# First attention: a planner's order for TensorE with a charge for changing between rounded and full-precision matmuls, and a hold

## The chip, the cores and the metric

The kernel runs on one core of a Trainium2 chip. The metric is device time in microseconds (us) of one execution, as the median over runs. The core has five engines that each execute their own list of instructions in order and wait for one another through semaphores: TensorE (PE in the profile, with its weight loads as PEld), VectorE (DVE), ScalarE (ACT), GpSimd (POOL) and SyncE (SP), which here issues DMAs.

## The reference

The program is two transformer-like layers over 2048 tokens of 256 features. Six steps follow each other: a routed feed-forward, the first attention, a routed feed-forward, a mixed feed-forward, a second attention, a mixed feed-forward. The change touches only the first attention (latent attention with 16 heads, causal):

```
q = (_rmsnorm(x @ w_q_a, q_a_ln) @ w_q_b).reshape(b, s, H, DQ)
ckv = x @ w_kv_a
...
kv = (_rmsnorm(c_kv, kv_a_ln) @ w_kv_b).reshape(b, s, H, DN + DV)
...
scores = jnp.einsum('bqhd,bkhd->bhqk', qf, kf) * scale
scores = jnp.where(mask[None, None], scores, jnp.finfo(scores.dtype).min)
p = jax.nn.softmax(scores, axis=-1)
o = jnp.einsum('bhqk,bkhd->bqhd', p, v).reshape(b, s, H * DV)
return o @ w_out
```

with s = 2048, H = 16, DQ = 192. The kernel folds the key and value weights into the query and output weights, so that all heads share one key of 128 features (64 latent, 64 rotated) and one value of 64 latent features.

## The kernel before, in words

`latent_heads` (L910) works on the 16 heads as 8 pairs. For each pair the queries are cut into 8 units of 256 queries for both heads, that is 512 columns (`LATENT_UNITS`, with `LATENT_CHUNKS` as the order of the chunks of 512 queries). A unit with number j has j + 1 steps, one for each 256 keys; the last is on the diagonal. Over all units there are 64 units and 288 steps (`LATENT_STEPS`, `FIRST_STEP`).

What happens to a step g:

- `scores`: TensorE computes two key tiles x 512 queries into one of two score banks (two PSUM banks each). Each tile is three products of *rounded* operands (type fp32r, high and low parts: L998, L999, L1003), and on the diagonal a product in bf16 that adds the mask (L1001).
- `max`: VectorE takes the running maximum over the steps of a unit (L1232). `evac`: ScalarE copies the scores to one of 12 held slots in SBUF (`HELD_STEPS`, L1108), which frees the score bank. `scores` of step g waits for `evac` of step g - 2; `evac` of step g waits for `max` of g, and for `values` and `sum` of step g - 12, which leave the slot.
- When all steps of a unit have their scores, TensorE turns the maxima (`turn_max`, L1020), VectorE reduces them (L1268), TensorE spreads them (`spread`, L1027). Then for each step VectorE subtracts them (`add`, L1279), ScalarE takes the exponential (`exp`, L1114), TensorE multiplies with the latent values (`values`, L1014: two matmuls on fp32 data in *full precision*, four records in the trace), and GpSimd adds up the sums (`sum`, L1208).
- After the last step of a unit ScalarE and VectorE drain the output bank; after each second unit TensorE does `sums` (L1033), `turn_sums` (L1039), `spread_inverse` (L1044) and two `project` (L1053), with steps of ScalarE and VectorE between them. All these are full-precision matmuls or transposes of fp32 data.
- `query` (L1062) makes the queries of a chunk for one head: five rounded products. `turn_q`, `turn_kv`, `fold_query` and `fold_out` (L1068 to L1091) make the weights of a pair, 8 times, from what SyncE has loaded.

The kinds in `SIDE` share two PSUM banks in turn.

The order of all this on each engine comes from `latent_plan` (L794). It lists every event with its engine, an assumed duration, a rank (its due time, counted in steps), and the events it waits for. `scores` of step g has rank g, `values` of step g has g + 11 (`SECOND_PASS_AFTER`), `add` and `exp` 10.0 and 10.4 later than g, `query` 7 steps before its first use, the weights 22 steps before. `turn_max`, `spread`, `sums`, `turn_sums`, `spread_inverse`, `project` and the drains have rank -1000 (`urgent`). Then it plays the work through: for each engine it looks for the earliest time at which any waiting event may start, takes among those that may start at that time the one of lowest rank, and of the engines' choices the earliest. The lists that come out are what each engine's block executes, in that order, with real waits on semaphores; the assumed times are used for nothing else. The choice is these lines of the planner:

```
first = min(at for at, _ in starts)
choices.append((first, min((nodes[e][2], e) for at, e in starts if at <= first + 0.001)[1], engine))
```

TensorE's list has 960 events: 288 `scores`, 288 `values`, 64 `query`, 64 `turn_max`, 64 `spread`, 32 each of `sums`, `turn_sums` and `spread_inverse`, 64 `project`, and 32 for the weights.

## Time and profile before

| | us |
|---|---|
| median of 3 runs | 1963.35 (1956.11 to 1963.68) |
| the profiled execution | 1954.15 |
| its span, first to last instruction | 1952.4 |
| TensorE busy in the span | 1731.2 (89%) |
| VectorE busy | 1529.0 (78%) |
| ScalarE busy | 1179.7 (60%) |
| GpSimd busy | 983.2 (50%) |
| mean granted clock of TensorE | 0.933 of 2.4 GHz |

The first attention's heads are planned as one stage, from about 150 to 1216 us of the span. A barrier of all engines ends it.

How to read the views: the page cuts the span in 40 slices and gives the busy share of each engine in tenths. The table by stretches gives busy time and number of instructions of each engine in a stretch. The timeline lists instructions in order of start, with the start, the duration and, in brackets, the idle time of the engine just before and what ended it; neighbouring ones of a line are merged into one row with a count. Matmuls are pipelined, so their durations overlap: the time that one takes from the engine is the distance from its start to the start of the next.

### The profile page before, as it was taken

To read this page: it belongs to the slowest core of one execution; us is meant where nothing else is said; L and a number is where in the kernel's file an instruction comes from. 1 tells how busy PE (TensorE), PEld (TensorE's weight loads), DVE (VectorE), ACT (ScalarE), POOL (GpSimd) and SP (SyncE) were. 2 spreads that over 40 slices of the span, in tenths; PEclk is the share of its full clock that TensorE was granted. 3 is DMA by queue.
4 is the path that set the end of the run, shared out by engine and by line. 5 is a ranking of instruction groups with operands and counts; after the bars stand their busy time and mean duration, and the time that the engine had idled before them with its cause. 6 is when DMAs were issued, how large, how long until landed. Compare 5 with 4: busy or idle time off the path is not lost. (4 is left out here: it accounts for less than half of the span.)

```text
span 1952.4 us, 27188 instructions
## 1 busy us (share of the span) xinstructions
PE 1731.2 (89%) x9368; PEld 1005.0 (51%) x9368; DVE 1529.0 (78%) x2236; ACT 1179.7 (60%) x2043; POOL 983.2 (50%) x820
## 2 busy tenths in 40 slices
PE   4667899999999999999999997557978999999996
PEld 3544555555555565565555653456644444444445
DVE  6763888998898888988889887776658888887716
ACT  1145787776876777777778774111323577777760
POOL 0004798897896988979879886011401000010110
PEclk8786999999999999999999999677968899999988
DMA  3200000000000000000000000111430200200001
GB/s 100 63 16 24 1 1 1 15 1 15 1 1 15 1 6 10 1 15 1 0 7 1 1 1 3 45 46 38 97 55 2 33 2 2 34 2 2 2 2 43
DMA packets 26697, 34.34 MB, mean 18 GB/s; under 512 B 5312, under 2 KB 19648, under 8 KB 26432
## 3 DMA queue, kind: packets, MB, share of 16 engines
q1 hardware_dynamic: 25360, 31.28, 6.7%
q8 instruction: 76, 1.25, 0.3%
q10 hardware_dynamic: 1200, 1.31, 0.2%
q14 instruction: 61, 0.50, 0.1%
HBM read 26.03 MB, written 6.29 MB: 17 GB/s over the span
## 5 line engine op out<-in xcount | busy, mean ns | idle before, releaser
L1208 POOL TENSOR_TENSOR lath_summed<-lath_summed,lath_held 128x512 f32<-128x512 f32 x392 | 524.8, 1339 | 54.4 <-ACT lath_held L1114 27.5
L1922 ACT ACTIVATE atth_probs<-atth_score 128x512 f32<-128x512 f32 (+3 forms) x640 | 293.3, 542 | 156.4 <-PE atth_score L1841 154.1
L1279 DVE TENSOR_TENSOR lath_held<-lath_held,lath_shift 128x1024 f32<-128x1024 f32 (+2 forms) x352 | 331.2, 968 | 24.6 <-PE lath_shift L1027 15.0
L1108 ACT ACTIVATE lath_held<-lath_score 128x1024 f32<-128x1024 f32 (+2 forms) x352 | 283.7, 828 | 105.1 <-DVE lath_largest L1232 51.5
L1881 DVE TENSOR_REDUCE atth_maxima<-atth_slot 128x2 f32<-128x1024 f32 (+3 forms) x288 | 285.9, 1041 | 53.5 <-PE atth_slot L1824 52.5
L1114 ACT ACTIVATE lath_held<-lath_held 128x1024 f32<-128x1024 f32 (+2 forms) x352 | 292.6, 861 | 48.7 <-DVE lath_held L1279 47.1
L1014 PE MATMUL lath_out<-lath_held,lat_latent 128*64 128x512 f32 (+1 forms) x1152 | 302.9, 591 | 8.0 <-ACT lath_held L1114 4.3
L998 PE MATMUL lath_score<-lath_query_hi,lat_key_hi 128*128 128x512 f32 x576 | 246.7, 428 | 22.8 <-ACT lath_held L1108 17.7
L1769 POOL TENSOR_SCALAR_AFFINE_SELECT atth_probs<-atth_probs 128x512 f32<-128x512 f32 x64 | 40.6, 635 | 433.9 <-ACT atth_probs L1922 433.9
L1003 PE MATMUL lath_score<-lath_query_hi,lat_key_lo 128*128 128x512 f32 x576 | 231.0, 401 | 0.0
L1232 DVE TENSOR_TENSOR lath_largest<-lath_score,lath_largest 128x1024 f32<-128x1024 f32 (+2 forms) x240 | 211.5, 881 | 17.6 <-PE lath_score L1003 12.6
L999 PE MATMUL lath_score<-lath_query_lo,lat_key_hi 128*128 128x512 f32 x576 | 219.8, 382 | 0.0
L998 PEld LDWEIGHTS lath_score<-lath_query_hi,lat_key_hi 128*128 128x128 f32 x576 | 108.8, 189 | 155.1 <-issue 80.7
L1214 POOL TENSOR_TENSOR lath_turn_a<-lath_query,lat_rope 128x512 f32<-128x512 f32 x64 | 86.4, 1350 | 190.5 <-DVE lath_turn_b L1285 155.7
L1854 PE MATMUL atth_out<-atth_probs,att_v_one 128*32 128x512 f32 (+3 forms) x1280 | 154.3, 556 | 0.6 <-POOL atth_probs L1769 0.5
L1003 PEld LDWEIGHTS lath_score<-lath_query_hi,lat_key_lo 128*128 128x128 f32 x576 | 110.4, 192 | 19.8
L1841 PE MATMUL atth_score<-atth_query,att_key 50*128 50x512 f32 (+3 forms) x384 | 116.4, 457 | 1.7 <-ACT atth_probs L1922 1.1
L999 PEld LDWEIGHTS lath_score<-lath_query_lo,lat_key_hi 128*128 128x128 f32 x576 | 109.3, 190 | 14.5
L1014 PEld LDWEIGHTS lath_out<-lath_held,lat_latent 128*64 128x64 f32 x1152 | 61.8, 135 | 92.4 <-issue 69.4
L1285 DVE TENSOR_TENSOR lath_turn_b<-lath_turn_b,lat_rope 64x512 f32<-64x512 f32 x64 | 76.7, 1199 | 31.1 <-ACT lath_turn_b L1141 29.5
L1841 PEld LDWEIGHTS atth_score<-atth_query,att_key 50*128 50x128 f32 x384 | 52.0, 190 | 92.3 <-ACT atth_probs L1922 86.2
L1224 POOL TENSOR_TENSOR lath_query_lo<-lath_query,lath_query_hi 128x512 fp32r<-128x512 f32 x64 | 83.7, 1308 | 15.3 <-ACT lath_query_hi L1148 15.3
(345 smaller groups left out, 2920.6 us busy)
## 6 DMA issues: line engine op xcount, KB each, us to landing
att_first_query<-att_scratch SPq DMA_DIRECT2D x12, 256.0 KB, 9.1
atth_query<-att_scratch SPq DMA_DIRECT2D x12, 256.0 KB, 8.9
ffn_a_w<-in_L_ffn_W SPq DMA_DIRECT2D x2, 1024.0 KB
lat_raw_out<-in_L_attn_w_out SPq DMA_DIRECT2D x8, 256.0 KB, 2.7
lat_rope<-in_c_rope_feature SPq DMA_DIRECT2D x1, 2048.0 KB, 10.8
ffn_b_w<-in_L_ffn_W SPq DMA_DIRECT2D x2, 1024.0 KB, 7.1
mix_a_factors<-in_L_ffn_factors SPq DMA_DIRECT2D x8, 256.0 KB, 4.3
att_scratch<-attp_high SPq DMA_DIRECT2D x4, 512.0 KB, 2.8
```

What stands on the lines that cost most here:

```text
L998: nc.tensor.matmul(scores, key_hi[:, keys], hi, start=True, stop=False)
L999: nc.tensor.matmul(scores, key_hi[:, keys], lo, start=False, stop=False)
L1003: last = nc.tensor.matmul(scores, key_lo[:, keys], hi, start=False, stop=True)
L1014: last = nc.tensor.matmul(by_head(out_bank[KL * i:KL * i + KL, :], q0), latent[:, kt, 0:KL], by_head(slot(n)[:, i, :], q0), start=(step == ...
L1108: nc.scalar.activation(part_columns(slot(n), tiles, q0), part_columns(score_bank[n % 2], tiles, q0), ACT.Copy)\
L1114: nc.scalar.activation(columns, columns, ACT.Exp, scale=SCALE0)\
L1208: nc.gpsimd.tensor_tensor(total, total, slot(n)[:, i, :], ALU.add).then_inc(s["tiles_summed"], 1)
L1232: nc.vector.tensor_tensor(out, first, second, ALU.max).then_inc(s["maxed"], 1)
L1279: nc.vector.tensor_tensor(columns, columns, added, ALU.subtract)\
L1841: nc.tensor.matmul(score_bank[u % 3][:, q0:CH], key_rows(GROUP * g + h, PLACED + 2, kt * P, P), query_rows(n, h, PLACED + 2, q0, CH - q0), ...
L1881: nc.vector.reduce_max(maxima[:, n % 2, :, pair, i, at], slot[r % 2][:, :, begin:begin + width], AX.X)\
L1922: nc.scalar.activation(probs[:, step % PROB_STEPS, h, q0:CH], score_bank[u % 3][:, q0:CH], ACT.Exp, scale=SCALE1)\
```

## The change

Only `latent_plan` and its constants change.

1. The planner knows two kinds of TensorE event: rounded (`scores`, `query`) and all others. It adds 0.2 us to an event of the others that comes after a rounded one, and 0.11 us to a rounded one that comes after another.
2. In the choice, an event of TensorE that changes the kind has its rank raised by 1.0 (`SAME_KIND`).
3. In the choice, TensorE takes the lowest rank among all events that may start within 0.6 us (`HOLD`) of the first that may, instead of among those that may start first. The other engines keep the old rule.
4. The assumed durations of TensorE's events are lowered: `query` 1.3 to 1.2, `spread` 0.55 to 0.45, `sums` 1.1 to 0.93, `turn_sums` 0.5 to 0.42, `spread_inverse` 0.6 to 0.5, `scores` 1.45 and 1.35 to 1.4 and 1.2 (on the diagonal), `values` 1.0 to 0.93. `turn_max` (0.5), `project` (0.85) and the weights' steps keep theirs.

No instruction is added or removed. What may change is the order on every engine, since all are played through together, and with it which of the two shared banks a side event uses.

```diff
+ROUNDED = ("scores", "query")
+TO_ROUNDED, TO_WHOLE = 0.11, 0.2
+HOLD = 0.6
+SAME_KIND = 1.0
...
-        add("tensor", 1.3, due, ("query", n), ("split_low", p), of("low", n - 2), of("whole", n - 1))
+        add("tensor", 1.2, due, ("query", n), ("split_low", p), of("low", n - 2), of("whole", n - 1))
...
-        add("tensor", 1.45 if whole else 1.35, g, ("scores", g), ("low", 2 * (u // 2) + 1), of("scores", g - 1), of("evac", g - 2))
+        add("tensor", 1.4 if whole else 1.2, g, ("scores", g), ("low", 2 * (u // 2) + 1), of("scores", g - 1), of("evac", g - 2))
...
-        add("tensor", 1.0, late, ("values", g), ("exp", g), of("values", g - 1), of("fold", u - 1) if s == 0 else None)
+        add("tensor", 0.93, late, ("values", g), ("exp", g), of("values", g - 1), of("fold", u - 1) if s == 0 else None)
...
+    rounded = [True]
+
+    def change(event):
+        if nodes[event][0] != "tensor" or (event[0] in ROUNDED) == rounded[0]:
+            return 0.0
+        return TO_WHOLE if rounded[0] else TO_ROUNDED
+
+    def turn_of(event):
+        return nodes[event][2] + (SAME_KIND if change(event) else 0.0)
+
...
-                first = min(at for at, _ in starts)
-                choices.append((first, min((nodes[e][2], e) for at, e in starts if at <= first + 0.001)[1], engine))
+                first = min(at for at, _ in starts) + (HOLD if engine == "tensor" else 0.0)
+                event = min((turn_of(e), e) for at, e in starts if at <= first + 0.001)[1]
+                choices.append((may_start(event), event, engine))
         at, event, engine = min(choices, key=lambda c: c[0])
         waiting[engine].remove(event)
-        end[event] = free[engine] = at + nodes[event][1]
+        end[event] = free[engine] = at + nodes[event][1] + change(event)
+        if engine == "tensor":
+            rounded[0] = event[0] in ROUNDED
         order[engine].append(event)
```

## Rows read from the trace of the kernel before

**Rows 1.** Page, busy tenths in 40 slices: TensorE.

```profile
PE   4667899999999999999999997557978999999996
```

**Rows 2.** Stretches: length, busy us of PE, PEld, DVE, ACT, POOL; granted clock, DMA.

```profile
365.00:465.00 100.00, 96.40 (x456) 55.62 (x454) 88.12 (x108) 78.23 (x114) 93.53 (x75) 1.00 0.00 1
465.00:565.00 100.00, 96.81 (x454) 56.29 (x453) 92.23 (x110) 76.59 (x115) 84.62 (x66) 1.00 0.03 8
565.00:665.00 100.00, 95.88 (x462) 57.52 (x463) 85.09 (x105) 74.63 (x112) 82.89 (x66) 1.00 0.02 8
...
765.00:865.00 100.00, 98.76 (x485) 60.16 (x484) 89.73 (x114) 77.60 (x115) 89.57 (x72) 1.00 0.01 4
...
150.00:1216.00 1066.00, 1011.49 (x4748) 594.83 (x4748) 899.91 (x1120) 789.94 (x1175) 903.18 (x712) 0.98 0.02 5
```

**Rows 3.** Waits of TensorE, 265 to 1165 us: total, times, longest; first and last.

```profile
PE lath_score L998 <- ACT lath_held L1108: 12.6, 21, 1.4
...
PE lath_shift L1027 <- DVE lath_held L1279: 0.6, 1, 0.6
```

**Rows 4.** Timeline of TensorE: start, duration, instruction, count; query, scores, values.

```profile
754.49 0.40 PE L1062 MATMUL lath_side<-lat_qa_rest,lath_w_rest_lo 128*128 128x512 f32 x1
754.73 0.39 PE L998 MATMUL lath_score<-lath_query_hi,lat_key_hi 128*128 128x512 f32 x1
754.95 0.39 PE L999 MATMUL lath_score<-lath_query_lo,lat_key_hi 128*128 128x512 f32 x1
...
756.20 1.07 PE L1014 MATMUL lath_out<-lath_held,lat_latent 128*64 128x512 f32 x4
...
761.48 2.79 PE L1014 MATMUL lath_out<-lath_held,lat_latent 128*64 128x512 f32 x12
...
772.77 1.08 PE L1014 MATMUL lath_out<-lath_held,lat_latent 128*64 128x512 f32 x4
773.78 0.50 PE L998 MATMUL lath_score<-lath_query_hi,lat_key_hi 128*128 128x512 f32 x1
774.12 0.40 PE L999 MATMUL lath_score<-lath_query_lo,lat_key_hi 128*128 128x512 f32 x1
774.36 0.40 PE L1003 MATMUL lath_score<-lath_query_hi,lat_key_lo 128*128 128x512 f32 x1
...
775.38 1.08 PE L1014 MATMUL lath_out<-lath_held,lat_latent 128*64 128x512 f32 x4
```

**Rows 5.** Timeline of TensorE: transposes between scores.

```profile
718.48 0.40 PE L1003 MATMUL lath_score<-lath_query_hi,lat_key_lo 128*128 128x512 f32 x1
718.72 0.60 PE L1020 MATMUL lath_side<-square,lath_largest 128*128 128x128 f32 x4
719.15 0.60 PE L1039 MATMUL lath_side<-square,lath_out_t 128*128 128x128 f32 x4
719.51 0.48 PE L998 MATMUL lath_score<-lath_query_hi,lat_key_hi 128*128 128x512 f32 x1
719.82 0.39 PE L999 MATMUL lath_score<-lath_query_lo,lat_key_hi 128*128 128x512 f32 x1
```

**Rows 6.** Timeline: first and last change of kind of 582.

```profile
151.72 0.77 PE L1062 MATMUL lath_side<-lat_qa_hi,lath_w_hi 128*128 128x512 f32 x1 [2.72 <-DVE lath_w_rest_lo L1289]
...
1184.28 1.94 PE L1014 MATMUL lath_out<-lath_held,lat_latent 128*64 128x512 f32 x8
```

**Rows 7.** Timeline of ScalarE: the copy that frees a score bank.

```profile
754.89 1.00 ACT L1108 ACTIVATE lath_held<-lath_score 128x1024 f32<-128x1024 f32 x1
```

**Rows 8.** Timeline of TensorE: scores ahead of a projection.

```profile
786.40 0.48 PE L998 MATMUL lath_score<-lath_query_hi,lat_key_hi 128*128 128x512 f32 x1
```

**Rows 9.** Timeline of VectorE: what that projection reads.

```profile
786.24 0.69 DVE L1316 TENSOR_TENSOR lath_out_t<-lath_out_whole,lath_side 128x512 f32<-128x512 f32 x1
```

**Rows 10.** Waits of ScalarE, 265 to 1165 us: the largest.

```profile
ACT lath_held L1108 <- DVE lath_largest L1232: 46.5, 39, 3.0
```

More of the change, by code:

```diff
@@ L839, in latent_plan @@
         add("vector", 0.7, urgent, ("turn_max_out", u), ("turn_max", u))
-        add("tensor", 0.55, urgent, ("spread", u), ("turn_max_out", u), of("add", FIRST_STEP[u] - 1))
+        add("tensor", 0.45, urgent, ("spread", u), ("turn_max_out", u), of("add", FIRST_STEP[u] - 1))
         add("scalar", 0.6, urgent, ("drain", u), ("values", last), of("fold", u - 1))
@@ L843, in latent_plan @@
         if j % 2:
-            add("tensor", 1.1, urgent, ("sums", k), ("sum", FIRST_STEP[u] - 1), ("sum", last), of("project", k - 1, 1))
+            add("tensor", 0.93, urgent, ("sums", k), ("sum", FIRST_STEP[u] - 1), ("sum", last), of("project", k - 1, 1))
             add("scalar", 0.6, urgent, ("sums_out", k), ("sums", k))
-            add("tensor", 0.5, urgent, ("turn_sums", k), ("sums_out", k), of("widen", k - 1))
+            add("tensor", 0.42, urgent, ("turn_sums", k), ("sums_out", k), of("widen", k - 1))
             add("vector", 0.2, urgent, ("turn_sums_out", k), ("turn_sums", k))
             add("scalar", 0.6, urgent, ("widen", k), ("turn_sums_out", k), of("spread_inverse", k - 1))
-            add("tensor", 0.6, urgent, ("spread_inverse", k), ("widen", k), ("fold", u))
+            add("tensor", 0.5, urgent, ("spread_inverse", k), ("widen", k), ("fold", u))
             add("vector", 0.7, urgent, ("spread_inverse_out", k), ("spread_inverse", k), of("project", k - 1, 1))
```

## The prediction

> **What bounds the kernel now.** I read the 40 slices of the page first: TensorE (PE) is at nine tenths or more from the sixth slice to the 24th, the stage in which the changed planner's order runs [rows 1]. The table by stretches says it more sharply: TensorE is busy 95.9 to 98.8 us of every 100, with the granted clock at 1.00 of 2.4 GHz; VectorE reaches 92.2 and GpSimd 93.5 in one stretch each. Over the whole stage, 150 to 1216 us, TensorE is busy 1011 us of 1066, VectorE 900, GpSimd 903, ScalarE 790 [rows 2]. The waits of TensorE between 265 and 1165 us add up to 28.7 us in six rows, 12.6 of them for the copy that frees a score bank [rows 3]. So this stage is bound by TensorE, which executes its list in order: a microsecond taken from or added to that list is nearly a microsecond of the stage, as long as VectorE and GpSimd keep their room of 15%. The stage is followed by a barrier, so its length goes into the kernel's in full. The rest of the kernel is untouched.
>
> **What a change of kind costs.** The change charges 0.11 us for going to rounded matmuls and 0.2 us for going back. Inside a scores step the products start 0.23 to 0.24 us apart, so six take 1.40 us. Between two values steps the first gap is 0.34 and the step lasts 1.60 us (773.78 to 775.38) [rows 4]. A values step among others of its kind adds (2.79 - 1.08) / 2 = 0.86 us, from the row of three in a run; alone between rounded work it takes 1.01 us (772.77 to 773.78) [rows 4]. One round trip (to whole and back) therefore costs 1.60 + 1.01 - 1.40 - 0.86 = 0.35 us; taking the gaps as 0.235 each, 0.34. The planner's 0.31 is close. I use 0.34.
>
> The page "TensorE: Matmul & The Clock Gate" of the Trainium skill, section "Back-to-back issue gap", gives the warm start-to-start time of a matmul as its columns divided by 2.4 GHz plus 2.5 ns (216 ns for 512 columns), with no term for the kind that ran before. By it a round trip would cost nothing and the new order would have nothing to win. The trace disagrees: 0.34 against 0.23 us at a first product after values, and 0.22 at one after a query, which is rounded too [rows 4].
>
> **Not every change of kind costs this.** Transposes (maxima, spread, sums) count as whole in the plan. In the trace, scores are followed by four transposes after 0.24 us, which is no more than another product; the next four come 0.43 us later; scores then start 0.36 us after those, with a first gap of 0.31 [rows 5]. 0.36 plus 0.08 is 0.44, what a set of transposes takes anyway. A trip to transposes alone is thus worth about nothing, and the plan charges 0.31 for it.
>
> **How many changes go.** The order of before has 960 TensorE steps with 582 changes of kind, or 291 trips; the first and the last are [rows 6]. 52 of the 291 hold transposes alone. 518 of the changes lie between 265 and 1165 us. For that stretch I put the new rule to every boundary of two steps, with what had then finished on the other engines: take, of all that can start within 0.6 us of the first, the lowest due time, with 1.0 added where the kind changes. Where the trace changes kind, the rule would stay 163 times; where it stays, the rule would change 54 times. Examples: at 756.20 values run though the copy that frees the next score bank ended at 755.89 (754.89 + 1.00), so the rule takes scores [rows 4, 7]. Net 109 of 518 changes, scaled by 582/518 to 122 in the stage, 61 trips. Leaving out the share of free ones (52 of 291) gives 50 trips x 0.34 = 17 us. This looks one step ahead only. The other end: 257 times scores are followed by something not rounded, and at 83 of these ends the next score bank was already free, at 42 more within 0.6 us. If all 125 were joined, 125 x 0.82 x 0.34 = 35 us. Three scores in a row don't fit, as there are two banks, and a copy ends more than 1 us after the end of the step in between in 95 of the 257. I take 17, nearer to the count by the rule itself: urgent steps, two or three for each pair of scores, still break pairs.
>
> **What holding back adds.** The 0.6 us are not charged to anything: an idle engine is preferred to a ready step whenever something with a lower due time comes soon enough. Urgent steps (due -1000) always win. Example: at 786.40 scores start; the rule would have waited for the VectorE product that ends at 786.93 (786.24 + 0.69), 0.58 us of idle, for a projection [rows 8, 9]. In the stretch the rule adds idle at 83 boundaries, 24.2 us in all: 41 waits for scores (11.4 us), 40 for urgent steps (12.7 us), 2 for values. Scaled, 27 us. At other boundaries it takes a step that is ready where the trace waited, 14.5 us, scaled 16. Net +11 us. The bounds are +27 (nothing comes back, since each such wait recurs in another place) and 0 (an early turn of the maxima or the spread shortens the chain that the next additions wait for, and other waits go).
>
> **The durations.** The new ones are nearer to the trace: values 0.93 plus charges for 1.01 alone and 0.86 in a run, sets of transposes 0.42 to 0.5 for 0.44. In the old plan scores and values take 1.45 + 1.0 = 2.45 us, in the trace 1.60 + 1.01 = 2.61 [rows 4], so the old plan lets TensorE run ahead of what it does and chooses by readiness that doesn't hold. Of the 28.7 us of waits [rows 3] about 14 are left after the 14.5 above. I take half of these as such misfits, -6 us, between 0 and -14; this is the weakest term. All engines' orders come from the same planning run, so theirs move as well; the instructions and their number stay, as do the DMAs. SyncE loads the next weights 22 steps ahead, and no wait for a load stands among TensorE's [rows 3]; moving these by a step is hidden by that lead.
>
> **What lies behind a held step.** A held TensorE delays values, whose end frees one of 12 held slots; ScalarE's next copy waits for that slot, and behind this copy in its queue are the exponentials. Scores and values are 9 to 11 steps apart at 218 of 288 scores, so one or two slots are the reserve. Against it, waits for values are not among ScalarE's in the trace: its copies wait for VectorE's maxima, 46.5 us of the largest row [rows 10]. I take nothing for it; if the reserve goes, a pair of values put off costs up to 1 us each time.
>
> **Sum.** -17 + 11 - 6 = -12 us. The profiled execution has a span of 1952.4 us and took 1954.15 us, 9.2 below the median of 1963.35. 1954.15 - 12 = 1942, on the scale of the median 1951. All times below are on that scale. A measurement of this kernel can tell about 0.5% from no change, so faster means below 1953.5 and slower above 1973.2.
>
> **Rivals.**
> - Given back (1959): the trips go, the holds eat them. -17 + 11 and no better fit is -6, and -17 + 19 with half of the returned idle is +2; between them 1957 to 1965. For it: the two terms come from the same rule and nearly the same number of places. Against: the plan's 2.45 for 2.61 is a real misfit that the change mends. Chance 0.27.
> - The holds win (1977, between 1973 and 1982; slower): one mechanism, TensorE waiting up to 0.6 us, for the most part before urgent steps and scores, in an engine that is 96% busy. At +27 against -17 it is +10, 1973; with the savings at half, +18, 1981. It decides from the point at which the mean wait per trip saved exceeds 0.34 us; by the counts above that is 27 / 50 = 0.54 before any idle comes back. For it: the case of [rows 8, 9], and the plan buys transposes' trips, which are free, with real waits. Against: 16 us of present idle lie at boundaries where the rule has something ready. Chance 0.23.
> - Another engine takes the gain (1960): VectorE is at 92% in 465 to 565 us and GpSimd at 94% in 365 to 465 [rows 2]; if pairs of scores bunch their maxima, these show as waits for banks. Worth half of the forecast's 12 us, 1957, to all of it, 1963. Chance 0.06.
> - No charge exists (1968): what costs 0.11 is the first product of any group, whatever ran before. Then nothing is saved, and the holds and the fit give 11 - 6 = +5. The query followed by scores without a longer gap [rows 4] speaks against it. Chance 0.02. The Trainium skill's page named above would have it so.
>
> **How the numbers follow.** Faster as worked out has 0.42, with 1928 to 1953 as its own range: the full pairing (-35) with holds at +11 and a fit of -11 gives 1928. The range that should hold 8 in 10 goes from 1932 to 1976: into the slower case up to +13, and short of the full pairing. Faster 0.42; same 0.27 + 0.06 + 0.02 = 0.35; slower 0.23.
>
> **What would show it.** In the timeline of TensorE: changes of kind at about 460 (582 before), more rows of four values records turned to eight, scores in pairs without idle. In the waits: the sum for TensorE in the stretch near 34 us (28.7 + 11 - 6); if it is over 45, the holds have won. In the stretches, TensorE's busy share falls slightly while the stage ends at about 1204 us. If the waits of ScalarE for values appear, or those of TensorE for the score bank grow, the bunching is at work. I'd be wrong altogether if the changes of kind hardly fell, or fell by far more than pairs allow.

## The result, and the profile after

The changed kernel takes 2019.63 us (median of 4 runs, 2014.19 to 2021.34) against 1959.73 us for the kernel before on the same chip. The ratio is 1.0283, with a 95% interval of 1.0233 to 1.0334: slower by 55 us or so by the ratio, where 12 us of gain were forecast and 1976 us was the upper end of the range.

TensorE's line on the page and its tenths in 40 slices, of the kernel after; the last row is the granted clock:

```profile
PE 1752.5 (87%) x9368; PEld 1020.8 (51%) x9368; DVE 1530.9 (76%) x2236; ACT 1181.9 (59%) x2043; POOL 977.2 (48%) x820
...
PE   4668989999899899899998988556978999999996
...
PEclk8788999999999999999999999777978897999968
```

The row of nines of [rows 1] now has eights in it. The stretches of the kernel after (busy us of PE, PEld, DVE, ACT, POOL; granted clock) that answer to [rows 2], and the whole stage, which now runs from 143 to 1265 us:

```profile
365.00:465.00 100.00, 91.85 (x428) 53.87 (x428) 84.25 (x103) 74.53 (x113) 86.88 (x69) 0.97 0.00 1
465.00:565.00 100.00, 91.46 (x426) 54.93 (x425) 88.69 (x105) 75.20 (x113) 85.23 (x67) 0.98 0.03 8
...
765.00:865.00 100.00, 89.53 (x430) 53.21 (x429) 85.06 (x103) 75.42 (x113) 88.85 (x71) 1.00 0.00 1
...
143.00:1265.00 1122.00, 1022.03 (x4764) 606.27 (x4765) 900.62 (x1119) 794.73 (x1185) 897.32 (x712) 0.97 0.02 5
```

TensorE was busy 96 to 99 us of every 100; now it is 90 to 94, and it gets through 426 to 430 instructions where it did 454 to 485. No other engine has become the bound: over the whole stage all have lost share (VectorE from 84 to 80%, GpSimd from 85 to 80%). The waits of TensorE from 265 to 1165 us in the kernel after (total, times, longest):

```profile
PE lath_score L1015 <- ACT lath_held L1125: 24.0, 30, 1.8
PE lath_side L1037 <- DVE lath_largest L1249: 13.8, 21, 1.2
PE lath_out L1031 <- DVE lath_out_whole L1320: 10.6, 7, 2.3
PE lath_side L1050 <- POOL lath_summed L1222: 7.6, 12, 1.9
PE lath_side L1050 <- DVE x L1339: 4.7, 6, 0.8
```

The line numbers are 17 higher than before (L1015 is L998, the first product of scores). All ten rows together are 68.1 us; the six of before were 28.7 [rows 3], and the wait for the copy that frees a score bank has doubled. At the same time the changes of kind fell further than forecast, from 582 to 424: scores in pairs went from 14 to 75, values in runs of two or three from 28 to 58.

Where the 65.7 us between the two profiled spans (1952.4 and 2018.1) lie: the heads of the first attention, from the first to the last step of TensorE, take 1069.8 us before and 1121.8 after, 52 us. The other 14 us lie behind the stage, where no instruction differs: 739.1 and 753.0 us. The second attention, about 335 us behind the end of the first's heads in both, ran at different clocks. First before, then after, same columns:

```profile
1550.00:1850.00 300.00, 298.08 (x2054) 127.70 (x2052) 247.67 (x287) 221.61 (x473) 23.50 (x37) 1.00 0.05 7
```

```profile
1600.00:1900.00 300.00, 298.05 (x1995) 127.46 (x1991) 241.26 (x278) 214.35 (x459) 22.85 (x36) 0.96 0.05 7
```

TensorE is as busy in both, but does 2054 instructions in one and 1995 in the other, at a granted clock of 1.00 against 0.96. In the 17 profiled executions of all kernels with the same work, this rest took 739 to 760 us, and it was longer, in the main, the longer TensorE stood at the lower of its two clock levels (1.2 GHz) there: 179 us of it for 739.1, 196 to 203 for 743 to 749, 220 for 753.0, 241 for 759.5. A straight line through the 17 rises by 0.30 us for each us at the lower level. The profiled execution of before is the shortest of them. For causes I therefore compare the length of the stage, and use ratios for verdicts.

### The profile page after: what moved, and what is told of

The parts are those of the page before. It is cut to its first block and busy times, and to the rows that moved or that the text cites. A ratio compares the mean times of both kernels' runs of the same rounds, so it can differ in the third digit from the quotient of the medians.

```text
span 2018.1 us, 27185 instructions
## 1 busy us (share of the span) xinstructions
PE 1752.5 (87%) x9368; PEld 1020.8 (51%) x9368; DVE 1530.9 (76%) x2236; ACT 1181.9 (59%) x2043; POOL 977.2 (48%) x820
## 5 line engine op out<-in xcount | busy, mean ns | idle before, releaser
L1296 DVE TENSOR_TENSOR lath_held<-lath_held,lath_shift 128x1024 f32<-128x1024 f32 (+2 forms) x352 | 329.1, 969 | 24.9 <-PE lath_shift L1044 16.6
L1898 DVE TENSOR_REDUCE atth_maxima<-atth_slot 128x2 f32<-128x1024 f32 (+3 forms) x288 | 285.9, 1041 | 61.4 <-PE atth_slot L1841 60.2
L1015 PE MATMUL lath_score<-lath_query_hi,lat_key_hi 128*128 128x512 f32 x576 | 240.0, 417 | 36.4 <-ACT lath_held L1125 30.6
L1231 POOL TENSOR_TENSOR lath_turn_a<-lath_query,lat_rope 128x512 f32<-128x512 f32 x64 | 91.0, 1422 | 235.1 <-DVE lath_turn_b L1302 155.4
L1015 PEld LDWEIGHTS lath_score<-lath_query_hi,lat_key_hi 128*128 128x128 f32 x576 | 109.5, 190 | 155.9 <-ACT lath_held L1125 71.8
L1871 PE MATMUL atth_out<-atth_probs,att_v_one 128*32 128x512 f32 (+3 forms) x1280 | 161.3, 579 | 0.1
L1858 PE MATMUL atth_score<-atth_query,att_key 50*128 50x512 f32 (+3 forms) x384 | 122.0, 481 | 1.7 <-ACT atth_probs L1939 1.2
L1031 PEld LDWEIGHTS lath_out<-lath_held,lat_latent 128*64 128x64 f32 x1152 | 68.1, 139 | 108.6 <-issue 83.9
L1214 POOL TENSOR_TENSOR lath_summed<-lath_held 128x512 f32<-128x512 f32 x56 | 73.1, 1306 | 69.5 <-ACT lath_held L1131 69.4
L1841 PE MATMUL atth_slot<-att_key,atth_query 48*128 48x512 f32 (+3 forms) x352 | 87.6, 461 | 7.9 <-DVE atth_maxima L1898 7.1
```

What stands on the lines that cost most here:

```text
L1015: nc.tensor.matmul(scores, key_hi[:, keys], hi, start=True, stop=False)
L1031: last = nc.tensor.matmul(by_head(out_bank[KL * i:KL * i + KL, :], q0), latent[:, kt, 0:KL], by_head(slot(n)[:, i, :], q0), start=(step == ...
L1296: nc.vector.tensor_tensor(columns, columns, added, ALU.subtract)\
L1858: nc.tensor.matmul(score_bank[u % 3][:, q0:CH], key_rows(GROUP * g + h, PLACED + 2, kt * P, P), query_rows(n, h, PLACED + 2, q0, CH - q0), ...
L1898: nc.vector.reduce_max(maxima[:, n % 2, :, pair, i, at], slot[r % 2][:, :, begin:begin + width], AX.X)\
```

## The experiments

Two theories stood against each other. **Hold**: TensorE, which bounds the stage, is made to wait up to 0.6 us for a step of lower rank although another is ready. **Bonus**: pairs of scores and runs of values use up what is ready, and TensorE then has nothing. A third, added for fairness: the new durations by themselves mislead the planner. Most numbers below come from one table:

| kernel | ratio to before (95%) | stage, us | end of the plan, us | changes of kind | runs of values and sums | waits 265 to 1165, us |
|---|---|---|---|---|---|---|
| before | 1 | 1069.8 | 1080.0 | 582 | 254 | 29.5 |
| changed | 1.0283 (1.0233 to 1.0334) | 1121.8 | 1150.8 | 424 | 220 | 68.1 |
| e1_no_hold | 1.0068 (1.0040 to 1.0095) | 1084.5 | 1093.8 | 554 | 265 | 39.7 |
| e2_hold_only | 1.0222 (1.0162 to 1.0281) | 1113.4 | 1122.0 | 544 | 235 | 64.2 |
| e3_no_bonus | 1.0237 (1.0192 to 1.0281) | 1118.1 | 1142.4 | 582 | 259 | 63.3 |
| e4_durations | 1.0080 (1.0048 to 1.0111) | 1084.1 | 1075.2 | 582 | 260 | 32.3 |
| e5_hold_urgent | 1.0243 (1.0211 to 1.0276) | 1115.7 | 1134.0 | 590 | 270 | 53.3 |
| e6_hold_others | 1.0190 (1.0150 to 1.0230) | 1106.4 | 1125.4 | 508 | 218 | 61.4 |
| e7_hold_half | 1.0105 (1.0062 to 1.0147) | 1089.8 | 1099.3 | 542 | 258 | 40.3 |
| e8_jitter_up | 1.0012 (0.9980 to 1.0044) | 1066.9 | 1068.4 | 562 | 272 | 23.4 |
| e9_bonus_only | 1.0046 (1.0019 to 1.0073) | 1084.0 | 1081.3 | 582 | 262 | 33.5 |
| e10_jitter_down | 1.0036 (1.0003 to 1.0069) | 1076.9 | 1077.7 | 584 | 258 | 28.2 |
| e11_values_dearer | 1.0115 (1.0082 to 1.0148) | 1092.4 | 1107.3 | 556 | 266 | 40.4 |
| e12_break_even | 1.0133 (1.0094 to 1.0171) | 1094.3 | 1110.0 | 472 | 263 | 41.3 |
| e14_narrow_bonus | 1.0086 (1.0062 to 1.0111) | 1084.6 | 1067.3 | 574 | 240 | 35.9 |
| e15_jitter_up2 | 1.0057 (1.0024 to 1.0091) | 1081.0 | 1088.4 | 580 | 261 | 38.5 |
| e16_jitter_down2 | 1.0003 (0.9979 to 1.0028) | 1077.1 | 1076.8 | 584 | 262 | 29.7 |

The stage and the waits are read in one profiled execution each, over TensorE's timeline; the stage goes from the start of TensorE's first step to the start of its last, and the waits are the sums of its idle time. They come to 29.5 for before, a little more than the 28.7 of the waits view, which leaves out idle times of 0.15 us and less. Changes of kind and runs are counted in the planner's list for TensorE. The end of the plan is the last of the times that `latent_plan` itself gives to its events while it plays them through. All intervals but those of e8 and e16 leave out 1.

The column of the plan's end holds what the forecast could have had for nothing: the planner itself says that the changed order ends 71 us later than the order of before. Over the 17 kernels its differences to before and the measured ones of the stage have a correlation of 0.95. It is no good for small things: it has e4, e9 and e14 at -5, +1 and -13 us where the stages are all 14 to 15 us longer.

### The hold, the bonus, the durations

**e1_no_hold**

```diff
-HOLD = 0.6
+HOLD = 0.0
```

> The changed kernel with HOLD at 0: charge, bonus for the same kind and new durations stay. If the hold is the loss, this comes back to the kernel before, 1945 to 1970 us, with the waits of TensorE from 265 to 1165 us near 30 us again. If the bonus for the same kind is the loss (pairs of scores and runs of values use up what is ready), it stays over 1990 us with over 60 us of waits.

**e2_hold_only**: the changed planner with

```diff
-TO_ROUNDED, TO_WHOLE = 0.11, 0.2
+TO_ROUNDED, TO_WHOLE = 0.0, 0.0
-SAME_KIND = 1.0
+SAME_KIND = 0.0
```

and the durations of before.

> The kernel before with the hold of 0.6 us alone: no charge, no bonus, old durations. If the hold is the loss: 1990 to 2015 us, though the changes of kind stay near 580. If the bonus is the loss: 1955 to 1975 us.

**e3_no_bonus**

```diff
-SAME_KIND = 1.0
+SAME_KIND = 0.0
```

> The changed kernel without the bonus (SAME_KIND 0), hold and charges kept. If the hold is the loss: 2000 us or more, and above the changed kernel, as the savings of 79 round trips (some 25 us) are gone. If the bonus is the loss: under 1975 us.

**e4_durations**: the changed planner with charge, bonus and hold all 0, so that the new durations alone are left.

> The new durations alone: no charge, no bonus, no hold. Both theories expect 1950 to 1970 us. A third one, that the lower durations mislead the planner (TensorE looks cheaper than it is without the charges), expects 1975 us or more.

Measured: 1975.55, 2007.23, 2010.10 and 1977.10 us, with 1962.29 for before. The theory of the bonus falls three times: without it nothing comes back (2010), the hold alone costs 45 us (2007), and without the hold the loss is down to 13. e1 doesn't come all the way back, though: it was to end at 1970 us at most with waits near 30 us, and has 1975.55 and 39.7. Most of e3's expectation holds, but it isn't above the changed kernel; its stage is 4 us shorter, though the changed kernel has 158 changes of kind fewer. The hold-only kernel shows what a hold turns into; its waits of TensorE, same columns:

```profile
PE lath_side L1037 <- DVE lath_largest L1249: 15.4, 16, 1.9
PE lath_score L1015 <- ACT lath_held L1125: 14.2, 19, 1.8
PE lath_side L1050 <- POOL lath_summed L1222: 13.2, 11, 2.7
```

The maxima and the sums, both urgent, have gone from 3.8 and 7.9 us to 15.4 and 13.2. Only the maxima's are a mark of the hold: without it, in e1, the sums' waits are 17.7 us and the maxima's are gone. The third theory isn't clear yet: e4, with no hold, no charge and no bonus, loses 15 us, as that theory has it, and e1 loses 13.

### Which holds, and how long

**e5_hold_urgent** and **e6_hold_others** split the hold by what it is for:

```diff
-event = min((turn_of(e), e) for at, e in starts if at <= first + 0.001)[1]
+event = min((turn_of(e), e) for at, e in starts
+            if at <= soonest + 0.001 or (at <= first + 0.001 and nodes[e][2] < -500.0))[1]
```

for urgent steps, with `> -500.0` for the others; `soonest` is `first` without the hold.

> The changed kernel, but TensorE is held back only for urgent steps (rank -1000: maxima, spread, sums, projection); charge and bonus stay. The kernel without a hold took 1976, the one with it 2020. If every hold costs its idle time, whatever it is for, about half of the 44 us: 1990 to 2005. If holds for scores and values are the loss, 1970 to 1985.

> The counterpart: held back only for steps that are not urgent (scores, values, queries, weights). If every hold costs its idle time: 1990 to 2010, and this and the run for urgent steps add up to about the whole loss. If holds for urgent steps are the loss: 1970 to 1985.

**e7_hold_half**

```diff
-HOLD = 0.6
+HOLD = 0.3
```

> The changed kernel with HOLD at 0.3 in place of 0.6. If the loss comes from idle time by the number of holds times their length: a quarter of it, 1980 to 1992. If it comes from a hold at all, however short: near 2000 or over.

Measured: 2006.22, 1998.31 and 1982.75 us against 1960.42. The halves of the hold cost 31 and 22 us of stage over e1, the whole 37, so they don't add up as expected: perhaps idling at one sort of place costs less once TensorE is idle at the other, which no run here tests. (The first half's time is 1 us over its range, the second's is inside.) The hold of 0.3 costs 5 us of stage over none, a seventh of what 0.6 costs (37), and its time lies in the range expected of a loss by number times length.

### Does any other order lose as much?

**e8_jitter_up**, **e10_jitter_down**, **e15_jitter_up2**, **e16_jitter_down2** are the kernel before with 0.01 or 0.02 us added to or taken from every assumed duration of TensorE but that of scores on the diagonal, an order that is another one for no reason:

```diff
-        add("tensor", 1.3, due, ("query", n), ...
+        add("tensor", 1.31, due, ("query", n), ...
```

> The kernel before with 0.01 us added to each assumed duration of TensorE in the planner: an order that is another one for no reason. If the kernel before is an ordinary order, this stays within 5 us of it (1957 to 1968), and the 13 to 15 us that the kernels without a hold lose have a cause in the new numbers. If the kernel before is a lucky one among its neighbours, this loses 10 us or more (1972 or over), and so little says nothing of the durations or the charge.

> The kernel before with 0.01 us taken from each assumed duration of TensorE: the second order that is another one for no reason. With the first (0.01 added, 1963 against 1960) it tells how far an arbitrary order strays: within 5 us of before, the 15 us of the new durations have a cause; 10 us or more off, they need none.

> A third arbitrary order: 0.02 us added to each assumed duration of TensorE. The first two were 2 and 7 us over before (ratios 1.001 and 1.004), the kernels without a hold 10 to 15. If the order of before is better than its neighbours by chance or selection, this is over it too, by 2 to 20 us (1963 to 1982); if not, as often below as above.

> A fourth arbitrary order: 0.02 us taken from each assumed duration of TensorE. As for the third: 1963 to 1982 if the order of before is a good one among its neighbours, 1950 to 1962 if it is an ordinary one.

Measured: 1962.73 (against 1960.42), 1969.81 (against 1962.72), 1975.89 and 1966.10 (against 1962.28). By ratio they lose 0.12, 0.36, 0.57 and 0.03%; their stages are -2.9, +7.1, +11.2 and +7.3 us against before. The first lies where an ordinary order was expected, the second between its two cases, the last two where the order of before is better than its neighbours. So an arbitrary order costs some 6 us of stage on average, with a spread of as much (four orders, one profiled execution each), and a difference of 10 us between two orders says nothing of the rule that made them. **e11_values_dearer** is a deliberate one:

```diff
-        add("tensor", 1.0, late, ("values", g), ...
+        add("tensor", 1.15, late, ("values", g), ...
```

> The kernel before with the assumed duration of values raised from 1.0 to 1.15, so that scores and values together are 2.60 us as in the trace (2.61). If a plan that takes TensorE for cheaper than it is loses time (the new durations alone lost 15 us), this gains or holds: 1945 to 1962. If any other number loses, 1970 or over.

1983.80 us: with scores and values together as dear as in the trace, the order loses more (stage +23), not less. So nothing here supports the idea that a truer duration makes a better order: e4 lowered the durations and lost, e11 raised one and lost. But neither is a clean test of it. All assumed durations of TensorE in the plan of before add up to 998 us, against 989 for the same list by the medians of its steps (below); in e4, without the charges, they are 933, and in e11 1041. Part of each loss may be the arbitrary one.

### What the saved trips are worth

**e9_bonus_only**: the bonus of 1.0 alone, on the durations of before, with no charge and no hold.

> The kernel before with the bonus of 1.0 for the same kind alone: no charge, no hold, old durations. If pairs can form without a hold, changes of kind fall well below 582 and the time falls by some 0.3 us for each trip saved. If two scores are hardly ever ready at the same moment, the changes stay near 580 and the time near that of before, 1955 to 1970.

**e12_break_even**: HOLD 0, and the charge added to the start by which events are compared, so that TensorE waits for one of its kind only as long as a change costs:

```diff
+                starts = [(at + change(e), e) for at, e in starts]
                 first = min(at for at, _ in starts) + (HOLD if engine == "tensor" else 0.0)
```

> The changed kernel with a hold at its price: TensorE takes the event that starts soonest with the charge for a change of kind added to its start, so it waits for one of the same kind at most as long as the change costs (0.11 or 0.2 us). Its list has 472 changes of kind, 82 fewer than the kernel without a hold (554, 1976 us). If a trip saved is worth its 0.34 us here, 41 of them give 14 us: 1955 to 1967. If the trips saved are bought with other waits, 1975 to 1995.

e9 took 1973.14 us with 582 changes of kind, as many as before: without a hold the bonus saves none, since two events seldom may start at the same moment. (Only the count came as expected; the time is 3 us over the upper value.) e12 took 1986.12 us, with 82 changes fewer than e1 and 10 us more of stage. Its waits are much the same (41.3 against 39.7 us), so they don't explain where 41 trips at 0.34 us have gone. The column of runs does: e12 has 263 runs of values and sums, e1 has 265.

The clue lies in the time of single steps, from the start of one to the start of the next. I took the 13185 steps of 17 kernels that have no wait and no low clock beside them, and fitted each as a sum of its own kind, of the kind before it and of the kind behind it. Summed over whole trips, so that it doesn't matter at which end the price is booked, it gives:

| trip | extra, us |
|---|---|
| scores, values, scores | 0.35 |
| transposes, values, transposes | 0.29 |
| projection, values, projection | 0.34 |
| scores, transposes, scores | 0.01 |
| scores, projection, scores | -0.01 |

(The medians of single steps, put together in the same way, give the same within 0.02.) A projection is full-precision work like values, and costs nothing; values cost about as much among transposes and projections, where the kind in the plan's sense doesn't change, as among scores. What costs isn't going between rounded and full precision, it is going to values and back. The starts show it at both ends: whatever full-width step comes just before values takes 0.09 to 0.10 us more, the first values of a run 0.05 and the last 0.10. Sums and `fold_out` behave like values. These three have something of their own: their matmuls are 64 columns wide and run two at a time into two halves of a bank.

With the medians of single steps the whole list of an order can be added up, as it would run at the full clock without a wait: 989.2 us before, 972.4 changed, 990.1 for e1 and 987.0 for e12. So the 82 changes fewer of e12 are worth 3 us and not 14. Its 10 us more of stage are the lower clock, for the most part: TensorE stood there for 57 us of the stage, in e1 for 37.

The same sum for e3 is 988.0. The bonus thus took 16 us out of TensorE's list, from e3 to the changed kernel, and the stage is 4 us longer all the same: over the stage TensorE waits 8 us more and stands at the lower clock for 23 us more.

**e13_wide_values** takes that away in the kernel before: both matmuls of a values step are 128 wide and write the whole bank. What they add up isn't the attention's output.

```diff
-last = nc.tensor.matmul(by_head(out_bank[KL * i:KL * i + KL, :], q0), latent[:, kt, 0:KL], by_head(slot(n)[:, i, :], q0),
-                        start=(step == 0), stop=(step == j))
+last = nc.tensor.matmul(by_head(out_bank[:], q0), latent[:, kt, :], by_head(slot(n)[:, i, :], q0),
+                        start=(step == 0 and i == 0), stop=(step == j and i == 1))
```

> The kernel before, its order kept, with both matmuls of a values step made 128 columns wide into the whole output bank instead of 64 wide into one half each (what they add up is then not the attention's output, and a step takes about 0.86 us more; the time of the whole is not the point). A values step in a run (its distance to a following values step) against one that scores or transposes follow: 0.86 against 1.01 to 1.13 us in the kernel before. If the price of a trip belongs to the change between rounded and full precision, the last values of a run still costs 0.2 to 0.3 us more than one inside it, and the first gap in scores after it is 0.1 us longer. If it belongs to the end of a run of 64-column matmuls, which run two at a time, it falls to under 0.1 us, as after projections.

It was run once, in 2075.26 us. From its timeline of TensorE (start, duration, instruction, count):

```profile
870.11 1.88 PE L1014 MATMUL lath_out<-lath_held,lat_latent 128*128 128x512 f32 x4
871.43 0.79 PE L1062 MATMUL lath_side<-lat_qa_hi,lath_w_hi 128*128 128x512 f32 x1
872.06 0.40 PE L1062 MATMUL lath_side<-lat_qa_lo,lath_w_hi 128*128 128x512 f32 x1
...
872.99 1.88 PE L1014 MATMUL lath_out<-lath_held,lat_latent 128*128 128x512 f32 x4
874.70 0.60 PE L1027 MATMUL lath_shift<-square,lath_row_max 128*128 128x128 f32 x4
...
876.44 3.60 PE L1014 MATMUL lath_out<-lath_held,lat_latent 128*128 128x512 f32 x8
879.48 0.80 PE L998 MATMUL lath_score<-lath_query_hi,lat_key_hi 128*128 128x512 f32 x1
```

The run of two: the first takes (3.60 - 1.88) = 1.72. Followed by transposes a step takes 874.70 - 872.99 = 1.71. Followed by rounded work it takes 1.32, and the next gap, 872.06 - 871.43 = 0.63 instead of 0.23, holds the other 0.40: 1.72. Over the stage the medians are 1.717, 1.715 and 1.314 + 0.401. The price is gone, rounded or not, and at the other end too: transposes after scores take 0.435 us whether transposes or these values follow, where in the kernels with 64-wide pairs they take 0.53 ahead of values. With the 64-wide pairs the last values of a run, ahead of transposes too, take 1.01 alone and 0.96 behind others, against 0.91 and 0.86 for those that values follow. So the price belongs to going to 64-wide pairs and back, and the planner's two kinds are the wrong ones.

**e14_narrow_bonus** asks whether the right ones pay: no hold, no charge, the bonus for staying inside or outside of values and sums, durations as in the trace (`values` and `sums` 0.86, sets of transposes 0.43, `scores` 1.46).

```diff
-ROUNDED = ("scores", "query")
+NARROW = ("values", "sums")
...
-        if nodes[event][0] != "tensor" or (event[0] in ROUNDED) == rounded[0]:
+        if nodes[event][0] != "tensor" or (event[0] not in NARROW) == rounded[0]:
```

> The changed planner without hold and charge, with the bonus of 1.0 for staying inside or outside of values and sums instead of rounded or not, and durations as the trace has them. Its list has about 240 runs of values and sums against 255 before and 220 in the changed kernel. If a run saved is worth 0.27 us, that is 4 us, and if any new order loses 2 to 20 us against the one of before: 1960 to 1978. Under 1955 would say that the right kind pays.

1979.23 us, 1 us over the range, with 240 runs: 25 runs fewer than e1 at the same stage. By the medians of steps its list is 9 us shorter than e1's (980.7 against 990.1), which is inside what an arbitrary order moves, and TensorE stood at the lower clock for 54 us of the stage where e1 has 37. Whether the right kinds pay stays open; no order tried here beats the kernel before.

## Why the prediction was wrong

**The bound** was read rightly for time that is added: TensorE, saturated, in order, and idle time added to it lengthened the stage. For time that is taken away the runs don't bear it out: 16 us out of the list (changed against e3) and 9 us (e14 against e1) left the stage 4 us longer and as it was.

**The price of a trip.** The sum 1.60 + 1.01 - 1.40 - 0.86 is right arithmetic on one sequence, scores, values, scores, which holds both a trip to 64-wide pairs and a change of kind; the fit has 0.35 for 0.34. I saw that transposes alone are free and took that for an exception; it was the rule. (The list of before has 48 such trips, not 52; nothing hangs on it.) The trace of before had the rows that decide: values followed by transposes also take 1.01 us. The size came out right all the same, and by luck: 79 trips in the plan's sense went where I counted 50, and these at 0.34 would be 27 us, but only 34 runs of values and sums went with them. By the medians of steps the list went from 989.2 to 972.4 us, 17 us, as in the sum. So this gain was there, and was lost elsewhere. The section "Back-to-back issue gap" of the Trainium skill's page "TensorE: Matmul & The Clock Gate", which knows no term for the kind that ran before, was nearer to the truth on the kind than I was: round trips among full-width work cost 0.01 us or less in the trace, as that rule has it. For the 64-wide pairs the trace disagrees, since there the distance to the next depends on what follows (0.86 or 0.96 us).

**The hold** is the step that failed most. I had it at +11 us net, with 83 places and 27 us at the upper bound. The waits in 900 us went up by 39 us (29.5 to 68.1), over the whole stage by 45 (61.7 to 106.6). The count was made one step ahead on the timeline of before, in which TensorE had been kept fed. It can't see that a wait moves every later one, which the planner itself does when it plays the work through (its end moved by 71 us), and most of the new idle time isn't of the length that the hold allows: waits of up to 0.6 us went from 10.9 to 16.6 us, longer ones from 18.6 to 51.5 us (17 to 48 of them). A stretch of the kernel after shows how such a one looks (timeline of all engines, part; idle time and what ended it in brackets):

```profile
515.33 1.08 PE L1031 MATMUL lath_out<-lath_held,lat_latent 128*64 128x512 f32 x4
516.25 1.02 ACT L1125 ACTIVATE lath_held<-lath_score 128x1024 f32<-128x1024 f32 x1
516.26 1.44 DVE L1305 TENSOR_TENSOR lath_w_lo<-lath_w_query,lath_w_hi 128x256 fp32r<-128x256 f32 x1 [0.37 <-ACT lath_w_rest_hi L1194]
516.34 0.65 PE L1044 MATMUL lath_shift<-square,lath_row_max 128*128 128x128 f32 x4
516.92 1.08 PE L1031 MATMUL lath_out<-lath_held,lat_latent 128*64 128x512 f32 x4
517.62 1.50 DVE L1306 TENSOR_TENSOR lath_w_rest_lo<-lath_w_query,lath_w_rest_hi 64x256 fp32r<-64x256 f32 x1
517.93 0.50 PE L1015 MATMUL lath_score<-lath_query_hi,lat_key_hi 128*128 128x512 f32 x1
...
519.05 1.21 DVE L1249 TENSOR_TENSOR lath_largest<-lath_score,lath_held 128x1024 f32<-128x1024 f32 x1
519.19 0.40 PE L1020 MATMUL lath_score<-lath_query_hi,lat_key_lo 128*128 128x512 f32 x1
520.18 1.20 DVE L1296 TENSOR_TENSOR lath_held<-lath_held,lath_shift 128x1024 f32<-128x1024 f32 x1
520.34 1.02 ACT L1125 ACTIVATE lath_held<-lath_score 128x1024 f32<-128x1024 f32 x1 [1.21 <-PE lath_score L1020]
521.26 1.87 ACT L1131 ACTIVATE lath_held<-lath_held 128x1024 f32<-128x1024 f32 x3
521.41 0.69 DVE L1302 TENSOR_TENSOR lath_turn_b<-lath_turn_b,lat_rope 64x512 f32<-64x512 f32 x1
521.41 0.53 PE L1015 MATMUL lath_score<-lath_query_hi,lat_key_hi 128*128 128x512 f32 x1 [1.83 <-ACT lath_held L1125]
```

(515.33 to 516.34 is the 1.01 us of values ahead of transposes.) TensorE does its last values at 516.92 and one step of scores, number 97 of the plan, at 517.93. Its next step is scores 98, for which ScalarE must empty the bank of scores 96, and it idles 1.83 us until that is done at 521.36. The view puts ScalarE's own wait down to the scores, but those of 96 had long been done; what ended last was VectorE's maximum of 96, at 520.26, for which ScalarE's copy waits too. VectorE came to it late: from 516.26 to 519.12 it split the next pair's weights (L1305 and L1306), which takes 2.9 us here, and for which the plan assumes 0.7. The same wait of 1.82 or 1.83 us comes once in each of six periods from 384 to 1068 us, each time 2.3 us behind the end of that split. These six are 11 us, as much as the wait for the score banks has grown (12.6 to 24.0). In the kernel before the second product of the split takes up to 1.5 us too, but from the third pair of heads on no wait of TensorE follows it, perhaps because no two steps of scores in a row stand so close behind it. That holds cause more waits is shown by the runs; by which steps one hold leads to one long wait isn't, and no run here corrects the durations that the plan assumes for the other engines.

**The durations.** -6 us, between 0 and -14, was a guess with the wrong sign. Alone they cost 14 us of stage (e4), of which some 6 would be expected of any other order. e4 leaves the charges out, though; with charge and bonus, in e1, the stage is 15 us longer. The reason given for the gain doesn't hold for the list as a whole either: the plan of before takes TensorE's steps for 998 us together and not for less than the 989 that they take. I had named it the weakest term, but bounded it on one side only.

**What wasn't in the sum.** The order of before is better than most of its neighbours: of ten orders without the hold of 0.3 or 0.6 only one has a shorter stage. An edit of the planner's numbers is likely to give this up. Then the clock: TensorE stood at its lower level for 39.0 us of the stage before and 61.0 after, and behind the stage it stood there longer than in the profiled execution of before, which is 14 us of the 65.7 and is luck in the main, since the ratio over all runs leaves some 4 us for it.

**The rivals.** "The holds win" was the mechanism, with the right place. It had 0.23, and an end at +18 us. What it decided by, a mean wait of 0.34 us for each trip saved, was met: 45 us of added waits for 79 trips are 0.57. As an account, the stage has 45 of waits, 11 for half of 22 us more at the lower clock, 8 for 53 further waits at 0.15 each (last section), less 17 saved: +47 of the 52 measured; the other 5 stay open. "No charge exists" had 0.02: for the change of kind as such it was nearly right, but the time doesn't show it, as runs of values were saved too. The signs named beforehand did their work: the changes of kind fell as said (424, where 460 was said), and the waits of TensorE were 68.1 where over 45 was to mean that the holds have won.

## What to carry to other kernels

An engine that bounds a stage and executes in order must not be held idle for something better while anything is ready: price a hold at what it lets go, and don't estimate it one step ahead on a timeline where nothing was held, since lost time spreads through all engines that feed one another. Where a planner makes the order, ask it first when its own plan ends: here it said 71 us later, and the stage became 52 us longer. Before a planner is given a charge for some transition, measure that transition with each kind in front and behind, 64-wide and 128-wide apart, not only in the commonest sequence. Where a view names an engine that had long been done, look for the other one that the step waits for. And before an order is judged, run a few orders that differ for no reason: here they lie up to 11 us of stage apart from the one that was shipped, so a rule must be worth more than that to be seen.

## What the runs showed of the hardware

**Two 64-wide matmuls at a time cost on the way to them and back.** Values in a run take 0.86 us for two matmuls of 512 columns in full precision; the 128-wide ones take 1.72. A trip to them and back costs 0.29 to 0.35 us more, whatever full-width work lies around, and for the 128-wide ones it costs nothing (-0.01 and -0.03 us among scores and among transposes in e13).

**A wait costs more than its idle time.** After a wait the first two products of scores are 0.34 us apart even where scores came before, instead of 0.23. The steps on both sides of a wait together take 0.15 us more than without one, on average over some 1000 waits of 17 kernels; that is beside the idle time itself.

**Single waits under 2 us were followed by the lower clock, but it cost little here.** The granted clock in four stretches of the kernel after, each just after a wait of 1.5 to 1.8 us (the last one behind a wait of 1.54 us at 559.45):

```profile
385.20:388.60 3.40, 3.40 (x10) 1.37 (x10) 3.40 (x4) 3.09 (x6) 3.11 (x3) 0.50 0.00 0
521.80:525.20 3.40, 3.40 (x10) 1.81 (x10) 3.37 (x4) 3.09 (x5) 2.73 (x3) 0.51 0.00 0
794.80:798.20 3.40, 3.38 (x14) 1.53 (x14) 3.35 (x4) 3.09 (x5) 2.43 (x3) 1.00 0.03 7
```

```profile
559.90:563.30 3.40, 3.03 (x17) 1.75 (x14) 3.37 (x6) 2.07 (x3) 3.40 (x3) 1.00 0.00 0
```

0.50 is 1.2 GHz: ten matmuls where fourteen go otherwise. It doesn't follow every such wait: the six waits of the period end at (the second row is the next product after the first wait)

```profile
384.44 0.50 PE L1015 MATMUL lath_score<-lath_query_hi,lat_key_hi 128*128 128x512 f32 x1 [1.83 <-ACT lath_held L1125]
384.78 0.39 PE L1016 MATMUL lath_score<-lath_query_lo,lat_key_hi 128*128 128x512 f32 x1
...
521.41 0.53 PE L1015 MATMUL lath_score<-lath_query_hi,lat_key_hi 128*128 128x512 f32 x1 [1.83 <-ACT lath_held L1125]
657.76 0.51 PE L1015 MATMUL lath_score<-lath_query_hi,lat_key_hi 128*128 128x512 f32 x1 [1.82 <-ACT lath_held L1125]
794.82 0.50 PE L1015 MATMUL lath_score<-lath_query_hi,lat_key_hi 128*128 128x512 f32 x1 [1.83 <-ACT lath_held L1125]
931.16 0.66 PE L1015 MATMUL lath_score<-lath_query_hi,lat_key_hi 128*128 128x512 f32 x1 [1.82 <-ACT lath_held L1125]
1067.62 0.59 PE L1015 MATMUL lath_score<-lath_query_hi,lat_key_hi 128*128 128x512 f32 x1 [1.83 <-ACT lath_held L1125]
```

and the one at 794.82 was not followed by it. The five periods between them last 136.97, 136.35, 137.06, 136.34 and 136.46 us and hold 2, 1, 2, 0 and 1 such falls of 3.4 us. A period with one fall is thus up to 0.1 us longer than the one with none, and those with two 0.6 to 0.7, though each fall slows TensorE by about 1.7 us (half of 3.4, an estimate): in an order with 10 us of idle time in each period TensorE probably waits a little less for it. So the 11 us for the clock in the account above are what TensorE spent, not what the stage would win back at the full clock. Behind the stage, with the second attention in it, where TensorE is busy 99% of the time, it cost more: 0.30 us for each us at the lower level, over 17 executions.
